# Attention inside a decoder layer: products by V between a unit's scores and its transposes

## What is computed

```python
qkv = (x @ Wqkv + bqkv).reshape(B, L, 3, n_heads, head_dim)
q, k, v = (qkv[:, :, 0], qkv[:, :, 1], qkv[:, :, 2])
scores = jnp.einsum('bqhd,bkhd->bhqk', q, k) / math.sqrt(head_dim)
scores = scores + slopes[None, :, None, None] * bias[None, None]
probs = jax.nn.softmax(scores, axis=-1)
out = jnp.einsum('bhqk,bkhd->bqhd', probs, v).reshape(B, L, D)
return out @ Wout + bout
```

## Time and profile before

| | |
|---|---|
| median of 3 runs | 3335.37 us (3334.26 to 3336.85) |
| the profiled execution, its own time | 3327.31 us |
| span in that profile | 3325.7 us, 57653 instructions |
| PE busy over the span | 3059.6 us (92%) |
| DVE busy | 2327.6 us (70%) |
| ACT busy | 1806.2 us (54%) |
| GpSimd busy | 1072.7 us (32%) |
| mean granted TensorE clock | 0.974 |

### The profile page before, as it was taken

The page is one execution under the profiler, slowest core; times in us unless marked ns, Lnnn a source line. Parts: engine busy times, 40 slices in busy tenths (PEclk is TensorE's granted clock), DMA queues, the critical chain, the costliest instruction groups (busy, mean ns, idle before and its releaser), DMA issues. The chain is left out here.

```text
span 3325.7 us, 57653 instructions
## 1 busy us (share of the span) xinstructions
PE 3059.6 (92%) x19234; PEld 2293.6 (69%) x19234; DVE 2327.6 (70%) x4173; ACT 1806.2 (54%) x3126; POOL 1072.7 (32%) x949
## 2 busy tenths in 40 slices
PE   6999799999999999789997899899999999768887
PEld 5777577777777777577775777688888888634443
DVE  5563688888888888645563699845555444589996
ACT  3332699999999999523222323232222222159995
POOL 3333422232232232234442356531111110016666
PEclk9999899999999999899999899999999999889999
DMA  6774422222232232446643644421111110301212
GB/s 209 240 256 177 111 78 62 77 86 65 63 95 66 63 98 65 138 171 213 229 165 130 182 140 138 145 97 45 45 43 42 43 45 23 118 7 55 67 45 76
DMA packets 239349, 350.51 MB, mean 105 GB/s; under 512 B 31792, under 2 KB 129104, under 8 KB 239184
## 3 DMA queue, kind: packets, MB, share of 16 engines
q1 hardware_dynamic: 208256, 290.41, 27.2%
q0 software_dynamic: 8912, 32.82, 3.0%
q10 hardware_dynamic: 22016, 25.17, 2.1%
HBM read 210.68 MB, written 137.64 MB: 105 GB/s over the span
## 5 line engine op out<-in xcount | busy, mean ns | idle before, releaser
L913 DVE CUSTOM_DVE_ANT_0 attend_probs<-attend_scores,attend_bias_table 128x1024 f32<-128x1024 f32 x512 | 622.7, 1217 | 110.6 <-PE attend_scores L754 100.3
L833 ACT ACTIVATE attend_probs<-attend_probs,attend_neg_max 128x1024 f32<-128x1024 f32 x512 | 592.5, 1157 | 89.1 <-DVE attend_neg_max L913 85.2
L770 PE MATMUL attend_turned<-ident,attend_probs 128*128 128x128 f32 x4096 | 548.9, 275 | 2.0 <-ACT attend_probsT L842 1.8
L770 PEld LDWEIGHTS attend_turned<-ident,attend_probs 128*128 128x128 f32 x4096 | 476.6, 140 | 90.7 <-ACT attend_probsT L842 14.9
L754 PE MATMUL attend_scores<-attend_k_stack,attend_q_stack 96*128 96x512 f32 x1024 | 368.2, 441 | 15.4 <-DMA attend_q_stack<-qk_parts 15.4
L842 ACT COPY attend_probsT<-attend_turned 128x512 f32<-128x512 f32 x640 | 356.8, 577 | 1.1 <-PE attend_turned L770 1.0
L2273 DVE TENSOR_TENSOR cross_ffn_h_lo<-cross_ffn_hidden,cross_ffn_h_hi 128x512 fp32r<-128x512 f32 x128 | 104.5, 822 | 337.3 <-ACT cross_ffn_h_hi L2164 336.6
L716 POOL TENSOR_TENSOR attend_out_parts<-attend_out_full,attend_out_parts 128x256 fp32r<-128x256 f32 x64 | 46.9, 733 | 754.5 <-ACT attend_out_parts L850 754.5
L785 PE MATMUL attend_out_acc<-attend_probsT,attend_v_in 128*32 128x256 f32 x4096 | 273.7, 385 | 0.7 <-DVE attend_out_full L933 0.7
L922 DVE COPY attend_probsT<-attend_turned 128x512 f32<-128x512 f32 x384 | 262.8, 684 | 2.2 <-PE attend_turned L770 2.1
L2161 ACT ACTIVATE cross_ffn_hidden<-cross_ffn_h_acc,cross_ffn_b_cols 128x512 f32<-128x512 f32 x128 | 88.2, 689 | 267.1 <-PE cross_ffn_h_acc L2068 243.6
(11 more groups left out here) (296 smaller groups left out, 6665.7 us busy)
## 6 DMA issues: line engine op xcount, KB each, us to landing
qk_parts<-qkv_qk_out SPq DMA_DIRECT2D x64, 512.0 KB, 3.2
attend_k_stack<-qk_parts SPq DMA_DIRECT2D x192, 128.0 KB, 2.5
attend_q_stack<-qk_parts SPq DMA_DIRECT2D x192, 128.0 KB, 2.7
qkv_wq_raw<-L_ffn_w POOLq DMA_DIRECT2D x16, 1024.0 KB, 7.8
o_parts<-attend_out_parts ACTq DMA_DIRECT2D x64, 256.0 KB, 2.5
carried_o_in<-o_parts SPq DMA_DIRECT2D x32, 512.0 KB, 6.4
qkv_x_in<-x SPq DMA_DIRECT2D x8, 1024.0 KB, 6.0
v_rows<-qkv_v_out SPq DMA_DIRECT2D x32, 256.0 KB, 3.4
```

The costliest lines, as they stand in the source:

```text
L770: last = pe.transpose(turned[:, bank, c], probs[:, i % 4, k * P:(k + 1) * P], ident[:, :])
L833: act.activation(probs[:, i % 4], probs[:, i % 4], ACT.Exp, bias=neg_max[:, i % 4:i % 4 + 1], scale=-1.0, accum_out=den[:, qg % 2, j, h:h ...
L913: dve.tensor_tensor_reduce(probs[:, i % 4], scores[:, i % 2], bias_table[:, h, at:at + T], -1.0, BIG, ALU.add, ALU.min, neg_max[:, i % 4:i ...
```

## The change

PE's order within a unit becomes `score(i + 3)`, `before(i)`, `turn_probs(i)`: the V steps of an odd unit, and the denominators' transposes, stand ahead of the unit's own transposes. So that the denominators keep their slot among the banks, DEN_UNIT becomes 2, and PE issues them at k = DEN_UNIT + 1 = 3, behind V steps 2 and 3 as before.

DEN_UNIT is also read in three other places. The banks become: unit 0: 0, 1; unit 1: 2, 0; unit 2: 1, 2; denominators 0; unit 3: 1, 2; unit 4: 0, 1; unit 5: 2, 0; unit 6: 1, 2; unit 7: 0, 1. The half that waits for `rdenT` is the first of unit 4 instead of the first of unit 5. And ACT's `copy_den` stands at k = 3 instead of k = 4: behind `exp(4)` and the copy of unit 2, ahead of `exp(5)` and the two copies of unit 3. The computation is the same, and so is the number of instructions.

```diff
-        DEN_UNIT = 3
+        DEN_UNIT = 2
         halves = [(k, x) for k in range(PER_GROUP) for x in range(2)]
         bank_of = {(k, x): (2 * k + x + (k > DEN_UNIT)) % 3 for k, x in halves}
         den_bank = (2 * DEN_UNIT + 2) % 3
...
                         if k % 2 == 1:
                             for c in range(k - 1, k + 1):
                                 times_v(turn, qg, c)
-                        if k == DEN_UNIT:
+                        if k == DEN_UNIT + 1:
                             turn_den(turn, qg)
 
                 def body(turn):
                     for i in range(UNITS):
                         if not (final(turn) and i + 3 >= UNITS):
                             score(*shifted(turn, i, 3))
+                        before(turn, i)
                         turn_probs(turn, i)
-                        before(turn, i)
```

## The result

| | before | after |
|---|---|---|
| median of 7 runs | 3334.26 us (3327.18 to 3336.85) | 3344.22 us (3341.41 to 3347.2) |
| ratio, 95% interval | | 1.0033, 1.0022 to 1.0045 |
| span of the profiled execution | 3325.7 us | 3340.9 us |
| first score product to first product of the next stage, in that execution | 355.10 to 1387.14, 1032.0 us | 354.57 to 1398.65, 1044.1 us |

The kernel is slower by 0.33%, some 10 us. In the profiled executions 12.0 us of the difference lie inside the attention stage; the rest of the 15.2 us between the two spans lies in stages that the change does not touch. The medians differ by 10.0 us only, so two single executions are compared here that lie a little further apart than the medians.

A forecast was written before the change was run, and what follows sets the result against it. PE was taken to set the attention stage's pace. Groups going from 15.92 to 16.00 us over 62 intervals were taken as +4 us on 3335.4, giving 3339 us, range 3311 to 3354.

The forecast's parts named there:

- the case with the highest chance: Main case: PE gains from the new order, but the den copy's wait on ACT outweighs it; +4 us, 3339, chance 0.50.
- PE alone: PE's attention order without waits for ACT: two units take 3.81 us instead of 3.87, a group 15.46, 0.46 less.
- rival B: Scores to V on PE costs only its lower bound, 0.54 us; group 15.64, -17 us, 3318; chance 0.11.
- The weight loads: Transposes' 140 ns loads on PE run under other transposes; only one behind V is exposed, costing 0.055 us more.
- rival D: Every transpose weight load on PE lies bare in both orders; two units stay at 3.87 us, +20 us, 3355; chance 0.07.
- ACT and the den copy: ACT idles about 1 us a group before copying the denominators, delaying exp(5) and unit 3's copies; PE loses 0.52 us.
- D + 2.51: Unit 4's second-half transposes start 2.51 us after the denominators' transposes start on PE; PE unhindered would be there at 2.05.
- Rival A: ACT wins its 0.5 us back and only PE's own time counts; group 15.46, -29 us, 3307; chance 0.14.
- The second place: Unit 0's transposes wait for ACT's copies of unit 7; late start absorbed, second half late by 0.02 us, group 16.00.
- Rival C: On ACT, exp follows a single copy 0.59 us later, not 0.47; group 16.16, +15 us, 3350; chance 0.18.
- the group: One round of eight units in the attention stage, forecast at 16.00 us against 15.92 before, over 62 intervals.
- The end of the stage: The last V steps wait for unit 7's copies instead of the output product; 0 to 1 us either way, taken as 0.

The follow-up runs named there:

- the four faster kernels: V ahead, denominators as before (0.9919 to before); the changed kernel with den copy behind exp(5) (0.9926), den ahead of V on PE (0.9912), or DVE copying unit 3 (0.9923).

## Why the prediction was right

It gave 3339 us, +4, and 0.37 to slower; the runs give 3344.2, about +10, inside the range. The range, 3311 to 3354, held a gain of 24 us as well, and none of the three outcomes had more than 0.37, so that the time fell inside says little. What says more is the mechanism: the case with the highest chance was the true one, and every wait of PE that it named is there. What was off is the size of the loss. (The lower end was to be half way from B to A; that is 3312.5, not 3311, which changes nothing.)

**PE alone.** 3.81 a pair was forecast and 3.81 to 3.83 measured; scores to V was taken at its upper bound 0.63 and is 0.63 to 0.64, so rival B falls. PE alone at 15.46 is nearly what the four faster kernels reach, 15.54 to 15.55. They are 0.38 us ahead of 15.92. Some 0.2 of it is cheaper switching, 4 pairs at 0.04 to 0.06, and the rest is the old wait of 0.22 at T(3), less the new one at T(0).

**The weight loads.** The changed kernel's pair of 3.81 us is what the sum with hidden loads gives; rival D, every load bare in both orders, would have kept 3.87. One sentence of the Trainium skill (TensorE: Matmul & The Clock Gate, Part 3: Packing small matmuls) lets a load overlap running matmuls only where the row group differs. The trace disagrees: every transpose has a load of its own of 140 ns, all on the same 128 rows, and yet the transposes start every 110 ns. The measurement decides.

**ACT and the den copy.** The idle time in front of it was put at about 1 us and is 1.07 in the group shown, 69.9 / 59 = 1.18 in the mean. D + 2.51 for T(4)'s second half is D + 2.51. Rival A, that ACT wins its time back, falls. One reading was wrong and cost nothing: the rest of ACT's free time was to go into waits for maxima, and the changed kernel shows none from 400 to 1360 us.

**The second place.** T(0) waits for unit 7's copy, as forecast, and the wait is not wholly absorbed: T(0) to the next scores takes 0.84 (809.07 to 809.91) against 0.79, 0.05 where 0.02 was given. Rival C falls: in the late stretch exp follows a single copy by 0.47 (803.27 to 803.74), not by 0.59.

**The term that was mis-sized** is the group, 16.00 for 16.09 in the mean, 16.10 in the one shown. Of that 0.10, 0.03 is T(0); the other 0.07 is spread over the 21 links between one den and the next, each taken to 0.01 us or so. Against a difference of 0.08 that was small for the sum and large for the answer. The scores of unit 7 beside the first den and beside the last stand at 382.36 and 1369.35 before and at 382.05 and 1379.60 after: 62 groups take 987.0 and 997.6 us, 10.6 us more instead of 5.

**The end of the stage** was taken as 0, within 0 to 1. It is 0.95: from that S(7) to the V steps of the last group, 1369.35 to 1377.02 before, 1379.60 to 1388.22 after. V waited there for the output product, and now waits for the copies of T(7). The kernel before, then the changed one:

```profile
1377.02 0.86 PE L785 MATMUL attend_out_acc<-attend_probsT,attend_v_in 128*32 128x256 f32 x12 [0.74 <-DVE attend_out_full L933]
```

```profile
1388.22 1.07 PE L785 MATMUL attend_out_acc<-attend_probsT,attend_v_in 128*32 128x256 f32 x16 [0.77 <-ACT attend_probsT L842]
```

With it 10.6 + 0.95 = 11.5 us of the 12.0 measured in the stage have a place. The other 0.5 lies ahead of the first of these groups (0.2) and behind the last V steps (0.3), and no run explains it.

## What to carry to other kernels

When a producer is moved later on one engine, look at where its consumer stands in the order of the other engine: everything queued behind a copy that now has to wait is late too. Here the price was paid where a buffer is freed behind it. A change of order that is a gain in itself can be lost by one constant that moves a second engine's step along with it, so time the two apart. And where the forecast difference per round is smaller than the rounding of its many links, take the links' sum from longer distances, or widen the chance of the other sign.

## What was not expected of the hardware

In the run that moved the den copy alone, 15 of the 62 groups took 19.3 us (as 802.81 to 822.15 from den to den) and the others 18.0 (as 822.15 to 840.15). The busy time by stretch of that kernel shows TensorE's granted clock (the column behind the engines) at 0.58 in one of them and full around it; the header first:

```profile
core 0: us, PE busy (x) PEld busy (x) DVE busy (x) ACT busy (x) POOL busy (x), PEclk, DMA share, GB/s
...
806.00:810.00 4.00, 4.00 (x26) 3.14 (x29) 2.46 (x4) 3.90 (x7) 0.00 (x0) 0.58 0.00 0
810.00:822.00 12.00, 12.00 (x116) 8.54 (x108) 10.36 (x19) 8.45 (x17) 0.73 (x1) 1.00 0.14 44
822.00:840.00 18.00, 16.34 (x151) 11.46 (x146) 14.14 (x26) 14.88 (x28) 0.73 (x1) 1.00 0.04 15
```

In shorter stretches it is 1.00 up to 805.5, 0.92 from 805.5 to 806, 0.50 from 806 to 809, 0.67 from 809 to 809.5 and 1.00 from there. So it fell to the lower of its two levels, 1.2 GHz, just ahead of 806 and rose to 2.4 GHz again between 809 and 809.5. What PE did before it fell, the first two rows, and at the lower clock, the last two:

```profile
803.00 0.72 PE L754 MATMUL attend_scores<-attend_k_stack,attend_q_stack 96*128 96x512 f32 x2
805.32 1.54 PE L770 MATMUL attend_turned<-ident,attend_probs 128*128 128x128 f32 x8 [1.60 <-ACT attend_probsT L842]
806.51 1.20 PE L754 MATMUL attend_scores<-attend_k_stack,attend_q_stack 96*128 96x512 f32 x2
807.51 1.91 PE L770 MATMUL attend_turned<-ident,attend_probs 128*128 128x128 f32 x8
```

It had waited 1.60 us and was some 0.6 us into the transposes. In the next group, 822 to 840, it waited the same 1.60 us and kept the full clock. The mean granted clock from den to den is 0.91 in each of the 15 groups of 19.3 us and 1.00 in each of the other 47, so the 1.3 us are the clock's. All of them have the same wait; why it fell in these and not in the others the runs do not tell. In the changed kernel, with waits of 0.5 us, the granted clock is 1.00 throughout from 400 to 1380 us.
